# First attention: the scores of a key block in one run over four row groups and four PSUM banks, with the orders of all engines laid out anew

## The reference

```
x = x + attn_a(norm(x))     # causal linear attention, 16 heads of 16, feature map elu(x)+1
x = x + ffn(norm(x))        # 256 -> 1024 -> 256, ternary weights, relu
x = x + attn_b(norm(x))     # windowed softmax attention (64 keys back), 16 query heads, 4 key heads
x = x + ffn(norm(x))        # the same ffn weights
```

## Time and profile before

| | |
|---|---|
| median of 3 runs (lowest to highest) | 3204.05 us (3196.79 to 3204.74) |
| the profiled execution's own time | 3207.31 us |
| its span, first to last instruction | 3205.5 us |
| PE busy, share of the span | 3056.6 us, 95% |
| DVE busy | 2326.1 us, 73% |
| ACT busy | 1813.0 us, 57% |
| POOL busy | 488.0 us, 15% |
| mean granted PE clock | 0.983 |

### The profile page before, as it was taken

How to read it: one execution, slowest core, us unless ns; L and a number is a source line. 1 busy time by engine, 2 the same in 40 slices (tenths; PEclk the granted TensorE clock), 3 DMA queues, 4 the chain that set the end, 5 groups by cost and what they waited for, 6 DMA issues and landing times.

```text
span 3205.5 us, 79515 instructions
## 1 busy us (share of the span) xinstructions
PE 3056.6 (95%) x27332; PEld 2430.5 (76%) x27332; DVE 2326.1 (73%) x5980; ACT 1813.0 (57%) x3717; POOL 488.0 (15%) x1048
## 2 busy tenths in 40 slices
PE   5789999999999999999999999999999999999977
PEld 4567778777778777778777777777777777777755
DVE  4467777777877777877777777777777777777654
ACT  1255555666655566555566555566555566655554
POOL 4011111111111111111011111011111011111110
PEclk8799999999999999999999999999999999999998
DMA  1000000000000000000000000000000000000000
GB/s 63 8 10 17 16 4 11 16 16 16 16 16 2 13 16 16 16 16 2 13 16 16 16 16 2 13 16 16 16 16 2 13 16 16 16 16 3 14 10 16
DMA packets 42116, 44.86 MB, mean 14 GB/s; under 512 B 2640, under 2 KB 41424, under 8 KB 42064
## 3 DMA queue, kind: packets, MB, share of 16 engines
q1 hardware_dynamic: 42064, 44.20, 4.5%
HBM read 21.12 MB, written 16.78 MB: 12 GB/s over the span
## 4 chain that ended last, share of the span: by engine, by line
PE 76%; DVE 11%; issue 6%; ACT 4%; POOL 1%; DVEq 0%; ACTq 0%; DMA 0%; POOLq 0%; SPq 0%
PE Q L374 15%; PE HID L424 12%; PE Y L445 12%; PE Q L565 9%; PE Q L833 4%; PE Q L603 4%; PE Q L598 3%; PE HID L382 3%; PE Q L847 2%; PE Q L616 2%; PE Q L580 2%; PE Q L767 2%; ACT f_hh L972 1%; DVE ff_xn L1295 1%; PE Q L854 1%
## 5 line engine op out<-in xcount | busy, mean ns | idle before, releaser
L971 ACT ACTIVATE f_r<-HID,b1c 128x512 f32<-128x512 f32 x512 | 353.1, 690 | 488.0 <-PE HID L424 364.8
L445 PE MATMUL Y<-w2t,f_hh 128*128 128x256 f32 x2048 | 542.3, 297 | 9.5 <-DVE f_hl L1309 7.2
L1309 DVE TENSOR_TENSOR f_hl<-f_r,f_hh 128x512 fp32r<-128x512 f32 x512 | 368.9, 721 | 238.4 <-ACT f_hh L972 236.7
L445 PE MATMUL Y<-w2t,f_hl 128*128 128x256 f32 x2048 | 512.6, 283 | 0.0
L424 PE MATMUL HID<-ff_xh,w1t 128*128 128x512 f32 x1024 | 430.4, 420 | 16.0 <-DVE ff_xl L1301 15.1
L445 PEld LDWEIGHTS Y<-w2t,f_hh 128*128 128x128 f32 x2048 | 389.2, 190 | 62.0 <-DVE f_hl L1309 27.7
L424 PE MATMUL HID<-ff_xl,w1t 128*128 128x512 f32 x1024 | 407.2, 398 | 0.0
L445 PEld LDWEIGHTS Y<-w2t,f_hl 128*128 128x128 f32 x2048 | 390.6, 191 | 4.1
L972 ACT ACTIVATE f_hh<-HID,b1c 128x512 fp32r<-128x512 f32 x512 | 351.9, 687 | 0.0
L1411 DVE TENSOR_TENSOR a_s<-Q,cst 128x512 f32<-128x512 f32 x512 | 328.4, 683 | 31.2 <-PE Q L565 25.8
L565 PE MATMUL Q<-a_qz,a_kT 32*128 32x256 f32 x2048 | 296.5, 407 | 2.8 <-DVE a_s L1411 2.8
(11 more groups left out here) (190 smaller groups left out, 7007.0 us busy)
## 6 DMA issues: line engine op xcount, KB each, us to landing
x<-in_x SPq DMA_DIRECT2D x32, 512.0 KB, 4.3
out<-x SPq DMA_DIRECT2D x32, 512.0 KB, 3.1
b_vm<-b_v SPq DMA_DIRECT2D x64, 96.0 KB, 2.1
x<-in_w SPq DMA_DIRECT2D x2, 512.0 KB, 8.0
a_s<-in_w_qkv SPq DMA_DIRECT2D x1, 768.0 KB, 4.5
ff_xn<-in_w SPq DMA_DIRECT2D x1, 512.0 KB, 9.4
f_r<-in_w SPq DMA_DIRECT2D x1, 512.0 KB, 10.2
cst<-in_const SPq DMA_DIRECT2D x1, 389.0 KB, 5.0
```

The source lines that it names most:

```text
L445: mm = pe.matmul(Y[t // 2][:, (t % 2) * D:(t % 2 + 1) * D], h[:, fb % 2, t * P:(t + 1) * P], w2t[:, fb, :], start=False, stop=(fb == FB - ...
L971: act.activation(f_r[:, fb % 2, :], HID[fb % 2][:], ACT.Relu, bias=b1c[:, fb:fb + 1]).then_inc(f_rr, 1)
L1309: dve.tensor_tensor(f_hl[:, fb % 2, :], f_r[:, fb % 2, :], f_hh[:, fb % 2, :], ALU.subtract).then_inc(f_lo, 1)
```

## The change

A key block's scores become one run, `scores(ch)`, over all four row groups, each writing a bank of its own: `Q[3], Q[0], Q[1], HID[1]`. The state sums move from `Q[3]` to `Q[2]`. Since HID[1] holds scores in phase 1, the FFN blocks of phase 1 all use HID[0] (`ONE_HID`), and each `up(fb)` there waits for the relu of block fb-1. `scores(ch)` waits for all four masks and the numerator evacuation of the block before; `scores(0)` for `own_norm_lo`. In phase 2, `up(5)` also waits for the masks of phase 1. The orders of PE, ACT, DVE and POOL in both phases are written anew.

```diff
+        A_SCORES = (Q[3], Q[0], Q[1], HID[1])
+        ONE_HID, TWO_HID = (HID[0], HID[0]), (HID[0], HID[1])
...
-                if fb >= 2:
+                if banks is ONE_HID:
+                    if fb:
+                        pe.wait_ge(f_act, turn * FB + fb)
+                elif fb >= 2:
                     pe.wait_ge(f_act, turn * FB + fb - 1)
...
-                    def scores(ch, pair):
+                    def scores(ch):
...
-                            pe.wait_ge(a_sm, a * 16 + 4 * ch + 2 * pair)
+                            pe.wait_ge(a_sm, a * 16 + 4 * ch)
+                            pe.wait_ge(a_ne, a * NT + ch)
                         for k in range(KB):
-                            for n in range(2):
-                                r = 2 * pair + n
+                            for r in range(4):
                                 rows = slice(32 * r, 32 * r + 32)
-                                mm = pe.matmul(Q[n][:, k * 2 * P:(k + 1) * 2 * P].rearrange("p (e q) -> p e q", e=2),
+                                mm = pe.matmul(A_SCORES[r][:, k * 2 * P:(k + 1) * 2 * P].rearrange("p (e q) -> p e q", e=2),
...
-                                    mm.then_inc(a_sc[n], 1)
+                                    mm.then_inc(a_sc[r], 1)
```

More of the change, by code:

```diff
@@ L409, in f_norm, with f_up @@
                 norm_transpose(ff, turn, HID)
-            def f_up(turn, fb, at_turn=None, blocks=range(KB)):
+            def f_up(turn, fb, at_turn=None, banks=TWO_HID):
                 if turn is None:
@@ L516, in up @@
                     def up(fb):
-                        f_up(own if fb < UPS else carry, fb, turn_b)
+                        f_up(own if fb < UPS else carry, fb, turn_b, ONE_HID)
                     def down(fb):
@@ L660, in phase1 @@
                     up(1)
+                    scores(1)
                     turn_numer(0)
-                    scores(1, 1)
-                    up(2)
[L664 to L671, removed]
+                    down(0)
+                    numer(1, 0)
+                    turn_y(0)
+                    numer(1, 1)
+                    project(0)
+                    scores(2)
+                    turn_numer(1)
+                    up(2)
+                    numer(2, 0)
+                    turn_y(1)
                     next_norm(0)
-                    turn_y(1)
-                    numer(2, 0)
                     numer(2, 1)
                     project(1)
-                    scores(3, 0)
+                    scores(3)
+                    turn_numer(2)
+                    next_norm(1)
                     down(1)
-                    turn_numer(2)
-                    scores(3, 1)
-                    next_norm(1)
                     turn_y(2)
@@ L685, in phase1 @@
                     project(2)
-                    qkv(s.b, 0, a + 1)
[L687 to L692, removed]
+                    up(3)
+                    turn_numer(3)
+                    down(2)
+                    turn_y(3)
+                    up(4)
+                    project(3)
+                    qkv(s.b, 0, a + 1)
                     qkv(s.b, 1, a + 1)
                     qkv(s.b, 2, a + 1)
+                    qkv(s.b, 3, a + 1)
                     down(3)
-                    qkv(s.b, 3, a + 1)
                 def phase2(s):
@@ L707, in up @@
                             pe.wait_ge(b_te, b * 12 + 3 * fb + 3)
+                        if fb == UPS and carry is not None:
+                            pe.wait_ge(a_sm, a_done * 16)
                         f_up(own if fb < UPS else carry, fb, turn_a)
@@ L885, in phase2 @@
                     numer(1)
[L886 removed]
                     up(0)
                     turn_numer(0)
+                    scores(2)
                     up(1)
+                    turn_y(0)
                     scores(3)
[L891 removed]
+                    turn_qk(2, 0)
                     numer(2)
+                    turn_qk(2, 1)
+                    turn_qk(2, 2)
                     down(0)
[L894 removed]
+                    project(0)
+                    down(1)
                     numer(3)
[L896 to L899 removed]
                     turn_qk(3, 0)
```

202 lines of the change are left out of this document (97 added, 105 removed).

## The result

The changed kernel takes **3158.38 us** (median of four runs, 3156.12 to 3163.23) where the kernel before took 3203.9 in four runs beside it: a ratio of 0.9868 (95% interval 0.985 to 0.9886), 45.5 us between the medians, and 1.3% by the ratio. The forecast was 3112 in a range from 3072 to 3185. The sign is right and the time lies in the wide range, but half of the 92 us that were forecast didn't come, and the time is outside of the narrower range that the forecast had for itself (3085 to 3145).

A forecast was written before the change was run, and what follows sets the result against it. PE was taken to bound both phases. The terms -136 - 10 + 70 - 22 + 6 = -92 us against 3207.3 gave 3115, and 3112 us for the median; range 3072 to 3185, the forecast's own 3085 to 3145.

The forecast's parts named there:

- Four groups in one run (-136): Phase 1 scores: four row groups together take 1.06 us for twice the work, removing 4.24 us a step, 136 in all.
- The third rival: Scores runs: four groups don't run at once, a run takes 2.12 us, kernel at 3226 us; chance 0.09.
- Waits in phase 1 (+70): PE in phase 1: new waits and hand-overs cost 2.2 us a step, 70 us in all.
- Work taken out (4.24 + 0.3): PE work in phase 1, per step: four scores runs of 1.06 us and three changes of shape of 0.10 removed.
- The wait of 0.6 at numer(0,1): Phase 1, first block: four masks outlast the work behind scores(0), so PE waits 0.6 us.
- that of `turn_y`: Phase 1, 37.5 us in: turn_y(2) waits 0.15 us for normalise(2), which stands between masks on DVE.
- The second rival: Phase 1: DVE's masking takes the gain back, waits 4.4 us a step, 3183 us; chance 0.17, shared with slow loads.
- Phase 2 (-22 + 6): Phase 2: earlier front gains 0.7 us a step (22 us); two more changes of shape later cost 0.2 (6 us).
- the 0.7 at down(6): Front of phase 2: down(6) waits 0.7 us because roots(1), 2.5 us, is ahead of low(6) on DVE.
- two changes of shape, 0.2: Later phase 2: scores(2) and numer(2) stand alone, adding two changes of the array's shape at 0.10 us each.
- up(5)'s wait for the masks: Phase 2: up(5)'s new wait costs nothing, since the masks ended some 12 us before.
- The bound of 1.44 for a run: Scores run: 16 weight loads in series at 0.09 us each take 1.44 us; kernel then at 3161 us.

The follow-up runs named there:

- experiment 3: Changed kernel with its new phase-2 orders up to numer(1), the old orders behind it and up(4) early on PE: 3136.98 us, ratio 0.9801.
- experiment 6: Changed kernel with the second pair of row groups waiting until the first pair's scores are complete: 3286.11 us, ratio 1.0266.
- experiment 1: Two crossed kernels: changed kernel with old phase-2 orders, 3159.71 us, ratio 0.985; second, kernel before with new phase-2 orders, 3246.7 us, ratio 1.0126.
- experiment 2: Changed kernel with the old phase-2 orders on all four engines, but up(4) early on PE: 3134.31 us, ratio 0.979.
- experiment 7: Changed kernel with each block's scores issued pair by pair, without a wait between the pairs: 3159.49 us, ratio 0.9855.

## Why the prediction was half right

**Four groups in one run (-136): right.** A run takes 1.08 for twice the work, and holding the pairs apart costs 128 us. The third rival is out. The Trainium skill's page "TensorE: Matmul & The Clock Gate", section "Measured speedup vs the span model", has 3.07 times for four row groups. The prediction's estimate from it (1.11) and its own figure (1.06) lie on both sides of the 1.08 measured.

**Waits in phase 1 (+70): right in kind, too small.** Work taken out (4.24 + 0.3) less the gain is 4.54 - 1.70 = 2.84 a step, against 2.2. The wait of 0.6 at numer(0,1) was there (0.46, 34 times, 16.0 us), that of `turn_y` was 0.29 in this step and 0.4 on average (13.7 us / 34), for 0.15. Halved masks take off 1.15 a step. The second rival, that DVE takes it back, names the right mechanism with the wrong size (4.4). Only 0.75 of the 2.84 is new idle time of PE (0.94 now, 0.19 before). The ends of matmuls are modelled in the profile, so short gaps can pass as busy. The distances between starts say where: the runs of scores fell from 8.59 to 4.31 us, while `up` and `down` grew by 1.20 together, numer by 0.81 and `turn_y` by 0.35, each counted up to the next call's start. What holds each of them up stays open beyond what the halved masks gave back.

**Phase 2 (-22 + 6): the step that failed.** The prediction said of the front: "By `up(0)` 0.9 is left; I take 0.7". Nothing is left. scores(0) began 6.91 into the phase and not 6.3, behind waits of 0.38 (down(5) for low(5)) and 0.48 (scores(0) for b_kT) that the prediction doesn't name. I had seen the 0.7 at down(6), but took it as a single hand-over after which PE keeps its lead. DVE works almost without a gap up to numer(0) (12.81 of 13.31 us), so PE's calls from down(6) on follow DVE's queue, whose length the new order didn't change. The 2.5 us of roots(1) that I named as the cause of a wait were part of the path itself. Crossing the front alone (42.70 with either) and moving low(6) show this. Behind numer(1) I had counted two changes of shape, 0.2; the new order there costs 0.57. By the timelines of experiment 3 the count of two was right and the price of 0.10 too low, if the shapes are all of it. 0.53 of it lie between numer(0) and scores(4), at the calls next to these changes, without idle time of PE, and the 29.97 from numer(0) on stay the same whether the front is 0.53 shorter or 0.25 longer. What stays open is how much is shape and how much short hand-overs to ACT that pass as busy: the one edit tried on PE alone saved 0.16 at the first change and then ran into a wait for ACT.

**The ends (nothing forecast of their own).** The forecast spread 92 us over 32 sequences alike, 2.87 each. The 29 steady steps gave 1.14 each: 1.73 less, 0.65 of it from phase 1 and 1.09 from phase 2, so 50 us were missed. Fill and tail gave 16.9 where three such steps would have given 8.6, which makes up 8. That is luck for the forecast, which had no term for it. That leaves 42, the whole error of the span (3113.5 forecast, 3155.5 found). The fill ran at a granted clock of 0.84 instead of 0.73. It isn't the packing that does it: with the pairs held apart (experiment 6) the same stretch is at 0.84 too and the third scores(0) starts at 227.0, and with only phase 2's orders changed (experiment 1, second kernel) at 0.70. The kernel of experiment 6:

```profile
45.00:130.00 85.00, 64.58 (x539) 49.89 (x540) 40.67 (x95) 22.41 (x40) 31.18 (x23) 0.84 0.03 7
```

So it comes with the rest of the new phase 1; which part of it, and whether the clock or the earlier calls come first, no run here tells. The time also lies in the wide range because its upper part was laid out for waits in phase 1; neither the loss in phase 2 nor the gain of the fill was in it.

**The remainder.** What was put down as free wasn't tested singly: up(5)'s wait for the masks doesn't appear in PE's waits. That of one FFN bank does appear once, where up(4) and up(5) meet (experiment 1). The changed kernel's early up(4) avoids it, and the prediction didn't name it as something that its new phase 2 buys: 0.71 us of phase 1 a step (51.79 against 51.08). Against the kernel of experiment 2 the rest of the new phase 2 loses 24 us.

## What to carry to other kernels

When a stretch is reordered, ask first which engine has no idle time in it: an earlier start on PE is worth nothing if that engine's queue is as long as before, and the wait then only moves from one name to the next. With that queue made shorter, the next engine's comes up, here ACT's. An order laid out anew is best costed and tried in pieces, since here one moved call was worth 0.71 us a step, and the rest of the same lists lost 0.57. And when a run is packed tighter, walk the engine that empties its banks: four masks of 0.60 behind a run of 1.08 set the first numer, though DVE was busy for only 41.55 of the phase's 51.15 us.

## What the runs showed of the hardware

- Row groups don't keep to the order of issue among each other. Issued pair by pair, the fourth group's matmul starts 0.04 us after the first's (experiment 7), and the time is the same. The Trainium skill's page "TensorE: Matmul & The Clock Gate", section "The mechanism", says that matmuls start and end strictly in the order of the program. For the starts of two-record fp32 matmuls on four row groups this trace differs, and the measurement decides.
- Four weight loads of 128 columns on four row groups go on beside each other: four in flight at once in the rows of L575. The run's steps are 0.32, 0.22 and 0.21 us. The bound of 1.44 for a run (loads in series, 0.09 each) doesn't apply.
- A run on two groups takes 1.06 us and one on four 1.08: both have four steps.
